# Projection 0 and the first feed-forward written as one program of 16 steps, with wo fetched and split inside attention 0

## What is computed

```python
x = x + jnp.tanh(g_xattn[0]) * _L0_xattn_ref(_layernorm(x), ctx_4096, L0_xattn_wq, ..., L0_xattn_wo, L0_xattn_ln_w)
x = x + jnp.tanh(g_ffn[0]) * _L0_ffn_ref(_layernorm(x), L0_ffn_W_base, L0_ffn_b_base, L0_ffn_enc0, ...)
x = x + jnp.tanh(g_xattn[1]) * _L1_xattn_ref(_layernorm(x), ctx_4096, ctx_4096, ...)
x = x + jnp.tanh(g_ffn[1]) * _L1_ffn_ref(_layernorm(x), L1_ffn_weight)
```

```python
return jnp.einsum('bqh,dh->bqd', out, wo)                  # _L0_xattn_ref
...
base = jnp.einsum('bsd,od->bso', x, W_base) + b_base       # _L0_ffn_ref
decoded = jnp.einsum('bsr,eor->ebso', e0, w0) + jnp.einsum('bsr,eor->ebso', e1, w1)
return base + real_fourier_orthogonal_multiply(decoded).sum(axis=0) * SCALING
```

## Time and profile before

| what | us |
|---|---|
| median of 3 executions | 1555.8 (1555.3 to 1561.07) |
| the profiled execution | 1561.66, its span 1559.9 |
| PE busy | 1411.1 (90% of the span) |
| DVE / ACT / POOL busy | 993.5 / 761.7 / 429.0 |
| context | 0 to 144 |
| attention 0 | 144 to 684 |
| from there to the first product of projection 0 | 684 to 708 |
| projection 0 | 708 to 906 |
| from there to the first product of the feed-forward | 906 to 937 |
| feed-forward 0 | 937 to 1131 |
| attention 1, and its prologue | 1131 to 1465 |
| feed-forward 1 | 1465 to 1560 |

### The profile page before, as it was taken

One profiled execution on the slowest core, in us unless ns is written; L12 is line 12 of the kernel. 1 busy time (PEld: TensorE's weight loads), 2 busy tenths in 40 slices (PEclk: granted clock), 3 DMA queues, 4 the chain that ended last, 5 costly groups with the idle time before them and its releaser, 6 DMA issues. The chain is left out here.

```text
span 1559.9 us, 29677 instructions
## 1 busy us (share of the span) xinstructions
PE 1411.1 (90%) x10918; PEld 1142.4 (73%) x10926; DVE 993.5 (64%) x1578; ACT 761.7 (49%) x1911; POOL 429.0 (28%) x467
## 2 busy tenths in 40 slices
PE   7997799999999999879999939999959999999478
PEld 6997798888988889657787728888736666666244
DVE  4362377677666776543323227787547999998687
ACT  4320277677666776742212101221127777777387
POOL 0010000101101010000101003243348888888324
PEclk9998899999999999989999969999979999999889
DMA  6643555365553652844554342200032222221013
GB/s 234 215 166 82 91 136 144 82 143 119 133 130 83 154 130 70 217 151 157 189 177 147 121 162 82 81 15 26 1 81 69 68 62 61 61 61 42 1 80 137
DMA packets 134277, 169.98 MB, mean 109 GB/s; under 512 B 28933, under 2 KB 106565, under 8 KB 134166
## 3 DMA queue, kind: packets, MB, share of 16 engines
q1 hardware_dynamic: 134166, 168.41, 38.4%
HBM read 84.84 MB, written 33.19 MB: 76 GB/s over the span
## 5 line engine op out<-in xcount | busy, mean ns | idle before, releaser
L1115 ACT ACTIVATE a_prob<-a_psS,a_negmax 128x256 f32<-128x256 f32 x512 | 237.0, 485 | 158.8 <-DVE a_negmax L1038 158.5
L1038 DVE TENSOR_REDUCE a_negmax<-a_psS 128x4 f32<-128x1024 f32 x128 | 154.4, 1207 | 70.8 <-PE a_psS L931 68.7
L860 POOL COPY a_recip<-a_recip_head 128x256 f32<-128x256 f32 x64 | 25.6, 400 | 531.7 <-DVE a_recip_head L1083 531.7
L941 PE MATMUL a_psT<-ident,a_prob 128*128 128x128 f32 x1024 | 137.5, 278 | 14.4 <-issue 6.0
L906 PE MATMUL a_psQ<-a_xT_hi,wq_hi 128*128 128x256 f32 x456 | 135.5, 297 | 0.4
L941 PEld LDWEIGHTS a_psT<-ident,a_prob 128*128 128x128 f32 x1024 | 116.4, 143 | 23.5 <-issue 12.6
L1132 ACT COPY a_probT<-a_psT 128x512 f32<-128x512 f32 x208 | 115.8, 609 | 34.5 <-PE a_psT L941 33.5
L906 PE MATMUL a_psQ<-a_xT_lo,wq_hi 128*128 128x256 f32 x456 | 127.8, 280 | 0.0
L906 PE MATMUL a_psQ<-a_xT_hi,wq_lo 128*128 128x256 f32 x456 | 127.7, 280 | 0.0
L1115 ACT ACTIVATION_READ_ACCUMULATOR a_prob<-a_psS,a_negmax 128x1 f32 x512 | 110.3, 216 | 0.0
L1290 PE MATMUL p_psY<-p_w_hi,p_o_hi 128*128 128x512 f32 x256 | 103.7, 405 | 2.5 <-DVE p_o_lo L1318 2.5
(11 more groups left out here) (234 smaller groups left out, 3524.3 us busy)
## 6 DMA issues: line engine op xcount, KB each, us to landing
a_q_stack<-a_q_hi SPq DMA_DIRECT2D x128, 128.0 KB, 2.7
a_q_stack<-a_q_lo SPq DMA_DIRECT2D x128, 128.0 KB, 2.9
c_raw<-lay_ctxT SPq DMA_DIRECT2D x16, 512.0 KB, 4.9
rows<-in_x SPq DMA_DIRECT2D x8, 1024.0 KB, 5.8
scratch_o<-a_oT SPq DMA_DIRECT2D x64, 128.0 KB, 2.1
p_o_lo<-scratch_o SPq DMA_DIRECT2D x8, 1024.0 KB, 5.5
p_x<-in_x SPq DMA_DIRECT2D x8, 1024.0 KB, 7.6
scratch_x<-p_x SPq DMA_DIRECT2D x8, 1024.0 KB, 4.0
```

The costliest lines, as they stand in the source:

```text
L860: nc.gpsimd.tensor_copy(recip[:, t % 2], recip_head[:, t % 2].unsqueeze(3).broadcast_to([P, TT, JH0, HD0])).then_inc(recip_ready, 1)
L941: last = nc.tensor.transpose(psT[:, kt, j * P:(j + 1) * P], prob[:, n % 2, j, kt * P:(kt + 1) * P], ident[:, :])
L1038: nc.vector.tensor_reduce(negmax[:, n % 2, :], psS[:, bank:bank + 2, :].rearrange("p a (j k) -> p (a j) k", k=S), AX_X, ALU.max, negate=Tr ...
L1115: last = nc.scalar.activation(prob[:, n % 2, j, :], psS[:, 2 * (n % 2) + j // 2, (j % 2) * S:(j % 2 + 1) * S], ACT.Exp, bias=negmax[:, n % ...
```

## The change

`proj0_stage` and `ffn0_stage` become one `mid_stage` without a barrier inside: 16 unrolled steps of 96 products, step s < 8 being batch s of the projection and step 8 + f batch f of the feed-forward. The first batch's normalisation and transposes stand inside step 7. `w_ffn` is built in steps 0 to 7 as before, from a `W_base` that is laid out transposed in HBM, so that nothing is transposed on PE; the low-rank part is 2 products in one pass, with high and low parts stacked over 120 partitions. `wo` also comes transposed (`woT`): its 8 blocks are loaded in attention 0's last two batches, POOL makes the high parts and DVE the low parts (`low_of_wo`) in the last batch, into the storage of `wq`, now called `wide`. The stream lies in the same place, and so is filled only after step 7. The first batch of attention output is loaded before attention 0 ends (`load_first_o`). `store_quad` is one DMA, with the row order of `woT` changed to fit. The last layer's weight is searched for its maximum in steps 8 to 11 and rounded in steps 12 to 15, without a clip; it goes to HBM and comes back in attention 1 (2 MB, ahead of `stack_query` in SP's queue). The two biases of attention 1 are laid out in HBM as columns, 2 DMAs without a wait.

```diff
+                o_rows = scratch["o"].rearrange("b (h t p) s -> b h p t s", h=HALF0, p=P)
+                sp.dma_start(o_rows[bass.ds(b, 1), h].rearrange("b p t s -> p (b t) s"),
+                             oT[:, QUAD * h:QUAD * (h + 1), :]).then_inc(o_stored[h], 16)
...
+            def load_wo(n):
+                if n >= 4:
+                    sp.wait_ge(rows.wo_split, n - 3)
+                sp.dma_start(rows.blocks[n % 4], c["woT"][n]).then_inc(rows.wo_loaded[n % 4], 16)
...
+                for h in range(2):
+                    sp.wait_ge(o_stored[h], 17)
...
                         for quarter in range(2, 4):
+                            load_wo(2 * quarter)
+                            load_wo(2 * quarter + 1)
                             sp.wait_ge(update_full, quarter - 1)
                             load_table(quarter)
...
+                    elif u == 0:
+                        sp.wait_ge(psQ_full, Q_USES * (B - 1) + XFILLS)
+                        for n in range(4):
+                            load_wo(n)
...
+                    else:
+                        load_first_o()
...
                             norm.rstd_of(pool, b + 2, rms=True)
+                        if final and u == 1:
+                            pool.wait_ge(psQ_full, Q_USES * B)
+                            pool.wait_ge(rows.wo_loaded[t % 4], 16 * (t // 4 + 1))
+                            nc.gpsimd.tensor_copy(wq.hi[:, t, :], rows.blocks[t % 4]).then_inc(rows.wo_high, 1)
...
+            def low_of_wo(n):
+                dve.wait_ge(rows.wo_high, n + 1)
+                nc.vector.tensor_tensor(wq.lo[:, n, :], rows.blocks[n % 4], plain(wq.hi)[:, n, :], ALU.subtract
+                                        ).then_inc(rows.wo_split, 1)
...
+                                low_of_wo(n // 2 - 1)
...
+def mid_stage(nc, sh, c, scratch, quant, w_out, w_ffn, rows, stream, x2_norm, attn1_bias):
...
+            def load_x1(f):
+                sp.wait_ge(x1_stored[f % 2], 16 * (f // 2 + 1))
+                sp.dma_start(first_rows(f), scratch["x1"][f].rearrange("(t p) d -> p t d", p=P)).then_inc(x1_loaded[f], 16)
...
+            def load_base(kt):
+                if kt < 2:
+                    sp.wait_ge(a_low, 4)
+                else:
+                    sp.wait_ge(tile_lo, 2 * (kt - 1))
+                sp.dma_start(rows.blocks[kt % 2], c["W_baseT"][kt]).then_inc(base_loaded[kt % 2], 16)
...
-                sp.dma_start(batch_of(x, b),
...
+            for s in range(B):
+                if s < KT - 1:
+                    load_base(s + 1)
+                if s == B - 2:
+                    sp.wait_ge(stacked, 64)
+                    load_x1(0)
...
+                    load_x1(1)
+                store_x1(s)
+                if s + 2 < B:
+                    load_o(s + 2)
+                    load_x(s + 2)
...
+            sp.wait_ge(rows_ready, 4 * (B + 2))
+            load_raw(1)
+            sp.wait_ge(wmax_done, KT)
+            load_raw(0)
+            for kt in range(KT):
+                store_rounded(kt)
+                if kt + 2 < KT:
+                    load_raw(kt + 2)
+            sp.wait_ge(w_stored, 16 * B)
+            sp.wait_ge(attn1_bias.loaded, 32)
...
+                    pool.wait_ge(quant.part_done, 1)
+                    nc.gpsimd.partition_all_reduce(quant.all_max[:, 1:2], quant.part_max[:, 1:2], P, ABSMAX
+                                                   ).then_inc(quant.all_done, 1)
...
+            def products(s, t, h):
...
+                if s:
+                    pe.wait_ge(rows_ready, 4 * (s - 1) + 2 * t + h + 1)
+                if s == B and t == 0 and h == 0:
+                    pe.wait_ge(tile_lo, 2 * KT)
...
+            def weight_tile(kt):
+                if kt == 0:
+                    pe.wait_ge(stacked, 64)
+                if kt >= 2:
+                    pe.wait_ge(full_ready, 2 * (kt - 1))
+                for h in range(2):
+                    nc.tensor.matmul(psT[:, 2 * (kt % 2) + h, :], enc_stack[0:STACK, kt * P:(kt + 1) * P],
+                                     update_stack[0:STACK, h * HALF_N:(h + 1) * HALF_N], start=True, stop=True
+                                     ).then_inc(tile_full, 1)
...
+            for s in range(STEPS):
+                for t in range(TT):
+                    for h in range(2):
+                        products(s, t, h)
+                        if s < KT - 1 and (t, h) == (0, 1):
+                            weight_tile(s)
+                        if s == KT - 2 and (t, h) == (1, 0):
+                            weight_tile(KT - 1)
+                        if s == B - 1 and (t, h) == (1, 0):
+                            transposes(0)
+                        if B <= s < STEPS - 1 and (t, h) == (0, 1):
+                            transposes(s - B + 1)
...
+            for s in range(B):
+                if s + 1 < B:
+                    low_of_o(s + 1)
+                dve.wait_ge(x_loaded[s % 2], 16 * (s // 2 + 1))
+                evict(s, 0, 0)
+                evict(s, 0, 1)
+                if s < KT - 1:
+                    full_tile(s)
+                if s == B - 1:
+                    moments(0)
+                    normalise(0)
+                evict(s, 1, 0)
+                if s == KT - 2:
+                    full_tile(KT - 1)
+                if s == B - 1:
+                    low_of_x(0)
+                evict(s, 1, 1)
+            moments(1)
+            normalise(1)
...
+            for f in range(B):
+                s = B + f
+                for kt in AT_START.get(f, ()):
+                    round_weight(kt)
+                dve.wait_ge(biased, TT * (f + 1))
+                for t in range(TT):
...
+                    if t == 1 and f + 1 < B:
+                        low_of_x(f + 1)
+                    if t == 1:
+                        for kt in IN_MIDDLE.get(f, ()):
+                            round_weight(kt)
+                    evict(s, t, 0)
...
+                    dve.wait_ge(rows_ready, 4 * s + 2 * t + 2)
+                    hold(dve, sh)
+                    last = x2_norm.stats_of(stream[:, f], t)
+                    if f + 2 < B:
+                        if t == 0:
+                            moments(f + 2)
+                        else:
+                            normalise(f + 2)
...
+                if f < QUANTISED:
...
+                for kt in AT_END.get(f, ()):
+                    round_weight(kt)
...
+            sp.dma_start(quant.weight[:, :, :], scratch["weight"].rearrange("k p d -> p k d")).then_inc(quant.weight_loaded, 16)
...
+            pe.wait_ge(quant.weight_loaded, 16)
...
-            x2_norm = StreamNorm(nc, es, "x2_norm", sh)
...
+        at = -(-nc.sbuf_base // 32) * 32
+        wide = SplitWeight(nc, es, "wide")
+        stream = nc.alloc_sbuf_tensor_at("stream", [P, B, TT, D], F32, offset=at)
...
+            with ExitStack() as held:
+                w_ffn = SplitWeight(nc, held, "w_ffn")
+                mid_stage(nc, sh, a, scratch, quant, wide, w_ffn, rows, stream, x2_norm, attn1_bias)
+        quant.weight = quant.sb("weight", [P, KT, D], BF16)
...
```

656 lines of the change are left out of this document (257 added, 399 removed).

## The result

The changed kernel takes 1506.7 us (median of 4 runs, 1506.0 to 1511.9) where the kernel before takes 1556.1 (4 runs, 1555.3 to 1561.1): a ratio of 0.9675, 95% interval 0.9653 to 0.9697. The prediction was 1498 with a range of 1485 to 1517. So it gains 49.5 us of the 58.3 that the sum promised. When the changed kernel was measured again later, two of its executions took 1992.6 and 2300.4 us at a mean granted clock of 0.65 and 0.56; they are left out of its median and its ratio there.

What follows compares the result with a forecast made beforehand. PE was taken to bound both stages, with PE mostly idle between them. From the profiled 1561.66 us, terms summing to -58.3 gave 1503.4; taking off the 5.9 above the median gave 1498 us, range 1485 to 1517.

Steps and rivals of the forecast that it cites:

- Two of the prediction's own signs of being wrong: PE waiting for rows or low parts in steps 12 to 15; a product's pitch having moved; no sizes given.
- joint 1: Attention 0's last PE instruction to the projection's first product: 6.6 us in the place of 24.5, -17.9.
- last batch: Attention 0's last batch: eight low parts added to DVE, 0.4 us taken for each, +3 (0 to +9.8).
- inside projection steps: Projection's eight weight tiles: one-pass products and no transposes, 2.0 us less each, steps of 22.3 us, -16.2.
- joint 2: Projection to feed-forward: work moves into step 7 beside PE's products, 31.1 us becomes 3.0, -28.1 (-29.4 to -22).
- warm-up ahead of step 8: Feed-forward's start: no idle time ahead, so no start at a lower clock, -1.6 (0 to -2).
- pitch of the product: Products, 0.2271 us in the projection and 0.2343 in the feed-forward: 0 taken, 5.5 us either way kept open.
- end and attention 1: Last feed-forward steps and attention 1: roundings +1.5, freeing semaphores +0.5, weight's 2 MB ahead of query stacks +0.5.
- DVE's chain in step 7: Evictions, moments, POOL's 1/sqrt and normalised rows take 17.6 us, so PE waits 1.25 us before the transposes.
- Rival D: Step 7: x1 read back late, or POOL's 17.56 us idle time comes again; 1522 us, chance 0.07.
- rival B: Last batch and steps 12 to 15: DVE held by POOL, low parts 3.3 us each; 1512 us, chance 0.15.
- Rival E: Projection steps: output loads queued behind x1 stores on SP land late, 11.7 us slack; 1573 us, chance 0.03.

Runs made afterwards that it cites:

- e4: Kernel before, with the first reduction over the partitions replaced by POOL copying each partition's own maximum; 1549.5 us (one run, beside a kernel before of 1563.0).
- e1: Changed kernel with POOL's reduction moved from the end of step 11 to behind step 12's bias addition; 1492.5 us, ratio 0.9555.
- e7: Changed kernel, three moves: reduction behind step 12's bias addition, update copy ahead of wo's low part, step 7's moments ahead of evictions; 1491.7 us, ratio 0.9556.
- e3: Changed kernel with the first reduction over the partitions replaced by POOL copying each partition's own maximum; 1494.5 us (one run).
- p1 to p3: Changed kernel with 32 bytes left free ahead of m_a_hi, of `wide` and m_a_hi, or of `wide` alone; 1516.7, 1518.3, 1507.4 us (one run each).

## Why the prediction held, and where it was off

The measured time lies in the range, and it is slower than the forecast's own 1489 to 1506. Two of the prediction's own signs of being wrong came: PE waits for low parts ahead of step 13, and the pitch of a product has moved. By its own steps, from the profiled executions (1561.66 and 1511.91, each some 5 us above its kernel's median):

| term | forecast | measured | how read |
|---|---|---|---|
| joint 1 | -17.9 | -17.7 | 24.5 against 6.8 |
| last batch | +3 | +2.9 | 683.72 to 689.05, less 2.4 of delay that was there when the batch began |
| inside projection steps | -16.2 | -15.5 | 197.4 against 181.9 (184.75 less the 2.8 of the transposes in step 7) |
| joint 2 | -28.1 | -28.3 | 31.1 against 2.8 |
| warm-up ahead of step 8 | -1.6 | -1.7 | 198.9 against 194.3, less the two rows below: a remainder |
| pitch of the product | 0 | -5.8 | 768 x 0.0076 |
| POOL's reduction | not in the sum | +12.1 | 9.33 of wait, 2.8 of clock |
| end and attention 1 | +2.5 | +1.9 | 428.9 against 430.8; 1.3 of it is the first load's wait, 8.74 against 7.48 |
| before the last batch | 0 | +2.4 | the first product of all 1.4 us later (13.02 against 11.57), and small drifts |

The measured terms add up to -49.7, the difference of the two executions. Those of the sum are each met within 1 us. **Joint 1** is 6.8 us where 6.6 was reckoned. **Projection steps** are 22.27 us (evictions at 744.04 and 766.31) where 22.3 was reckoned; the first weight tile waits 1.52 us for its stacked operand, which the -14.5 end of that term had room for. **Joint 2**: PE waits 1.09 us in step 7, forecast 1.25, and 16 transposes follow as forecast. The **last batch** is met in size only. The sum has 0.4 us for each of eight low parts; what came is 1.7 us of longer waits for the update copies and 2.8 of a lower clock, against a wait of 1.25 us for an early load that the kernel before has and the changed one has not:

```profile
645.63 0.74 PE L931 MATMUL a_psS<-a_k_stack,a_q_stack 128*128 128x256 f32 x4 [1.25 <-DMA a_q_stack<-a_q_lo]
```

Three sums of the prediction are off by a little. DVE's chain in step 7 adds up to 17.35 us and not 17.6 (11.8 + 2.47 + 0.3 + 1.24 + 1.54), so PE's wait would have been 1.0; 8 x 2.0 is 16.0 and not 16.2; and E's slack is 22.3 - 4 - 5.5 = 12.8 us and not 11.7. None changes the forecast by more than 0.3 us.

**The step that failed** is in the paragraph on joint 2. It listed POOL's idle time of 17.56 us as a part of the joint and priced POOL's 1/sqrt in the new place by the next batch's 1.24, which is right for the 1/sqrt. It never asked what the 17.56 were. They were the far side of the reduction (e4), and the change moves the reduction: the changed kernel has it behind step 11 (L1348 to L1350), ahead of a bias addition that DVE's evictions wait for. So the sum lacks a term, which measured +12.1. Rival D had named the gap and put it in step 7, where POOL has no reduction. The question that would have found it: which instruction stood ahead of an idle time without a releaser, and where does that instruction stand now.

**That the range held** owes something to chance: the missing +12.1 was partly paid by the faster product, -5.8, which the text had as 0 with both ends kept and without a cause. Without those 5.8 us the time would have been some 1512, still in the range, at rival B's number for another reason than B's.

**Rival B** did not come in the last batch. The eight low parts took 1.21 us each, POOL's casts 1.04:

```profile
L1068 DVE TENSOR_TENSOR wide<-rows,wide 128x1024 fp32r<-128x1024 f32 x8 | 9.7, 1212 | 0.0
L894 POOL CAST wide<-rows 128x1024 fp32r<-128x1024 f32 x8 | 8.3, 1043 | 0.0
```

By construction each waits for its own cast and is over before the next one, so no pair of them meets. The rule that the prediction cited from the Trainium skill, "SBUF — State Buffer", section on who interferes with whom (one port pair, held for a whole instruction), shows itself where they do meet, at the start of step 13, in the size that the earlier trace rows had; PE had no wait there:

```profile
1016.50 5.80 POOL L1344 TENSOR_TENSOR stream<-stream,m_later 128x1024 f32<-128x1024 f32 x2
...
1017.35 2.70 DVE L108 TENSOR_SCALAR m_later<-rows 128x1024 uint32<-128x1024 uint32 x1
1020.08 3.30 DVE L114 SCALAR_TENSOR_TENSOR rows<-m_later,rows 128x1024 f32<-128x1024 f32 x1
```

**Rival E** did not come: `m_a_lo` lands in 7.7 us (median), and no PE wait in steps 1 to 7 ends with it. The 2 MB of the weight ahead of the query stacks cost nothing that shows: the first scores waited 5.21 us where they waited 5.35.

## What to carry to other kernels

Before an idle time "without a releaser" is booked as a gain, find the instruction beside it that causes it, follow that instruction into the new order, and look at what is now queued behind it; a reduction over the partitions shut POOL for 13 us here, and belongs where POOL's next work is due much later. When work of three engines is fused, a cost that was in part hidden beside a barrier needs a new place where it hides. And when a stage is rebuilt, compare the start-to-start time of its products before and after: where the operands start was worth 10 us of 1507 in the changed kernel's two stages, though only 1.4 of the 49.5 us between the two kernels.

## What the runs showed of the hardware that was not expected

- POOL does nothing for 5.5 to 6.0 us ahead of and 6.9 to 7.5 us behind a reduction over the partitions of 0.41 us (changed kernel, e1, e7); with a plain copy in its place both are gone (e3). Ahead of the last stage the idle time stands only ahead of it (10.16 us), and a cast follows at once.
- In the changed kernel a 512-column product takes 0.2267 us when both operands in SBUF start at the same offset from a multiple of 64 bytes and 0.2333 us when one is 32 bytes off the other, at the same granted clock (p1 to p3). In another stage equal offsets gave 0.2325, so something else costs there too.
- In attention 0's last batch, where PE has many short waits, the granted clock fell behind one of 2.62 us in seven of eight profiles (to a mean of 0.76 to 0.87 over 660 to 670 us) and behind one of 1.5 us in none of the six others.
